# Four graph-attention layers on one core: the steps from elu to projection moved closer behind the scores

## The chip, the cores and the metric

The kernel runs on one core of a Trainium2 chip. The metric is the device time of one execution in microseconds. The median of three runs of the kernel before is 650.46 us (649.96 to 650.89). Engines are called as the profile calls them: PE (matmuls; PEld is its weight load), DVE (VectorE), ACT (ScalarE), POOL (GpSimd) and SP (SyncE, here only a queue of DMAs).

## The reference

`x` is 4096 x 64 and `adj` a 4096 x 4096 matrix of zeros and ones, dense in its first rows and columns and thin in the last. Four graph-attention layers follow each other. Cut to what matters:

```python
def layer(x, adj, W, a, slope):
    Wh = x @ W
    e = (Wh @ a_src)[:, None] + (Wh @ a_dst)[None, :]
    e = jnp.where(e > 0, e, slope * e)                 # leaky relu
    attention = softmax(where(adj > 0, e, -big), axis=1)
    return attention @ Wh                              # elu in layers 0, 2, 3; + bias in layer 1

for l in range(4):
    x = layernorm(x + elu_or_bias(layer(x, adj, W[l], a[l], slope[l])))
```

The layer norm has no weights, only mean, variance and a scaling of each row.

## The kernel before, in words

The first third of the program reads `adj` and makes for every tile of 128 rows a short list of the columns that occur in it: 85 chunks of 128 indices for 32 tiles, 12 chunks for tile 0, two or fewer new ones for each of the last twenty. A tile then attends only over its chunks. After that come the four layers, written out in full.

A layer works through 32 tiles (eight groups of four tiles) in rounds. The table `LAG` (L108) says how many rounds a step of a tile stands behind that tile's spread; a step of a group is done in the round in which its last tile is due. Every engine runs the same rounds in its own fixed order and waits on semaphores, so nothing overtakes on an engine:

- POOL, `gather` (L404): one indirect DMA for each chunk reads 128 rows of `table[l]` (the projected rows of this layer, in DRAM) into `xg`. 85 of them a layer. For layers 1 to 3, the 14 chunks called EARLY, which need rows of groups 0 to 4 alone, wait for `low_written` (the tables of groups 0 to 4); the other 71 wait for `written` (groups 5 to 7 as well). Layer 0's gathers are done during the first third.
- PE: `spread` (L572, L575) writes the scores of a tile into one of two banks and waits for the tile's gathers; `turn` (L588) transposes the exponentials; `aggregate` (L601) sums the rows; `turn_rows` (L457) and `project_rows` (L467) transpose a group of the new `x` and multiply it by the next layer's weights.
- ACT: `slope` (L716), `exponentials` (L725), `copy_turned` (L734), the elu's exponential `elu_part` (L738), `estimate_rstd` (L673, L675: a logarithm and an exponential), `copy_xt` (L667) and `copy_wh` (L660, from the projection's bank to SBUF).
- DVE: `mask_scores` (L1079, L1088), `combine` (L1103 to L1118: a group's division, residual and maximum), `norm_stats` (L1128 to L1139, the step "center"), `norm_rows` (L1147 to L1151, the step "scale"), and `slope` (L1068, the step "own"). At the start of each layer it also writes `lone_rows` in one long instruction (L1167).
- SP: as soon as a group's `copy_wh` is done, one DMA (L368) writes its rows to the next layer's table, in the order of the groups; in layer 3 it writes the result instead (L372).

In the text, "project(4)@33" means the projection of group 4 in round 33. Group g ends with tile 4g+3, so a group's step stands in round 4g+3+LAG. POOL's two waits for a layer:

```python
pool.wait_ge(low_written, 16 * l * LOW_GROUPS)
for c in EARLY:
    gather(l, TILES_OF_CHUNK[c][0], c, LOW * P)
pool.wait_ge(written, 16 * (1 + l * (GROUPS - LOW_GROUPS)))
```

## Time and profile before

| | us |
|---|---|
| median of three runs | 650.46 |
| the profiled execution, its own time | 652.01 |
| its span, first to last instruction | 649.0 |
| PE busy | 357.6 (55%) |
| DVE busy | 425.1 (66%) |
| ACT busy | 363.8 (56%) |
| POOL busy | 358.4 (55%) |

The profiled execution took 3.0 us more than its span and 1.55 us more than the median of the runs. The busy times are sums over stages of different kinds: the lists are made until about 217 us, layer 0 stands from there to about 298 us, and layers 1, 2 and 3 end at about 416, 533 and 649 us. In the slices of the page POOL is empty in layer 0, whose gathers are done by then, and works in seven to eight tenths of every slice of layers 1 to 3.

### The profile page before, as it was taken

How to read it: one execution, taken by the hardware profiler on the slowest of the kernel's cores; microseconds unless marked ns; L12 is line 12 of the kernel's file. 1: busy time of each engine (PE TensorE's matmuls, PEld its weight loads, DVE VectorE, ACT ScalarE, POOL GpSimd, SP SyncE). 2: the span in 40 equal slices, each digit the busy share in tenths (PEclk: the TensorE clock that was granted, in tenths of full speed). 3: DMA queues.
4: the chain of work that ended last, by engine and by line, in shares of the span. 5: the costliest groups of instructions: out<-in, count | busy, mean ns of one | idle time of the engine just before them, and what ended most of it. 6: DMA issues, size and time to landing. Idle time of an engine off the chain costs nothing.

```text
span 649.0 us, 10852 instructions
## 1 busy us (share of the span) xinstructions
PE 357.6 (55%) x3412; PEld 321.3 (50%) x3424; DVE 425.1 (66%) x1856; ACT 363.8 (56%) x797; POOL 358.4 (55%) x354
## 2 busy tenths in 40 slices
PE   2363322331222689872488787318866840796784
PEld 1243221221221689861477676217865830796673
DVE  2998979999999638992136567503566770346676
ACT  3574856777761379971176666206666730576563
POOL 0200574457675700017777774677777657777770
PEclk9999999999999999995599878659999875899787
DMA  7997999999981100001222221212212221222221
GB/s 269 429 380 274 369 377 408 423 413 409 410 311 19 23 5 2 27 29 42 27 28 29 36 36 35 53 26 28 29 29 44 42 52 25 28 29 35 45 43 30
DMA packets 22083, 86.73 MB, mean 134 GB/s; under 512 B 6851, under 2 KB 12102, under 8 KB 17798
## 3 DMA queue, kind: packets, MB, share of 16 engines
q1 hardware_dynamic: 10102, 73.40, 28.1%
q0 software_dynamic: 10880, 11.51, 12.4%
q10 hardware_dynamic: 1040, 1.08, 0.5%
q8 instruction: 30, 0.49, 0.3%
q14 instruction: 31, 0.25, 0.1%
HBM read 80.59 MB, written 5.37 MB: 132 GB/s over the span
## 4 chain that ended last, share of the span: by engine, by line
POOL 37%; DVE 15%; issue 14%; PE 5%; DMA 2%; ACT 2%; POOLq 0%; DVEq 0%; ACTq 0%
POOL xg L404 37%; PE bank L575 2%; DMA xg<-table,index 2%; PE bank L601 2%; DVE arena L1079 1%; DVE key L1106 1%; DVE nbr L879 1%; PE bank L588 1%; DVE penalty L999 1%; DMA table<-wh 1%; ACT arena L725 1%; DVE stats L1131 1%; ACT arena L716 1%; DVE key L866 1%; DVE top L856 1%
## 5 line engine op out<-in xcount | busy, mean ns | idle before, releaser
L404 POOL DMA_INDIRECT xg<-table,index x340 | 336.8, 990 | 191.4 <-issue 99.7
L1079 DVE CUSTOM_DVE_ANT_0 arena<-bank,arena 128x256 f32<-128x256 f32 (+3 forms) x144 | 71.4, 499 | 163.9 <-ACT arena L716 163.4
L716 ACT ACTIVATE arena<-bank,sloped_own 128x256 f32<-128x256 f32 (+3 forms) x144 | 76.9, 537 | 179.8 <-PE bank L575 179.2
L575 PE MATMUL bank<-packed,xg 128*128 128x128 f32 x744 | 120.0, 300 | 58.7 <-DMA xg<-table,index 56.9
L690 ACT ACTIVATE arena<-arena,half 128x4096 bf16<-128x4096 int32 x32 | 118.5, 3707 | 47.0 <-DMA arena<-in_adj_t 46.4
L575 PEld LDWEIGHTS bank<-packed,xg 128*128 128x128 f32 x744 | 112.7, 216 | 2.1
L601 PE MATMUL bank<-xg,arena 128*128 128x64 f32 x744 | 104.8, 279 | 0.0
L601 PEld LDWEIGHTS bank<-xg,arena 128*128 128x128 f32 x744 | 99.3, 202 | 2.0
L725 ACT ACTIVATE arena<-arena,neg_max 128x256 f32<-128x256 f32 (+3 forms) x144 | 80.7, 561 | 3.6 <-DVE neg_max L1088 3.6
L572 PEld LDWEIGHTS bank<-penalty,ident_b 128*128 128x128 bf16 x144 | 17.0, 118 | 116.8 <-DMA xg<-table,index 106.7
L588 PE MATMUL bank<-packed,arena 128*128 128x128 f32 x372 | 67.7, 290 | 10.7 <-ACT arena L734 8.2
L572 PE MATMUL bank<-penalty,ident_b 128*128 128x256 bf16 (+2 forms) x132 | 42.8, 324 | 48.8 <-DMA xg<-table,index 41.1
L398 POOL TENSOR_TENSOR colv<-word_f,packed 128x1024 f32<-128x1024 f32 (+4 forms) x10 | 21.5, 2149 | 82.1 <-DVE word_f L935 82.1
L497 PE MATMUL bank<-fix,ones_b 3*128 3x288 bf16 x32 | 13.2, 412 | 95.7 <-ACT arena L690 58.9
L734 ACT COPY arena<-bank 128x256 f32<-128x256 f32 (+3 forms) x144 | 59.7, 423 | 2.5 <-PE bank L588 2.5
L588 PEld LDWEIGHTS bank<-packed,arena 128*128 128x128 f32 x372 | 47.6, 150 | 14.3 <-ACT arena L725 13.9
L497 PEld LDWEIGHTS bank<-fix,ones_b 3*128 3x128 bf16 x32 | 3.2, 99 | 98.7 <-ACT arena L690 60.3
L467 PE MATMUL bank<-wx_pair,xt 128*128 128x132 f32 x128 | 30.3, 377 | 12.7 <-ACT wh L660 8.9
L499 PEld LDWEIGHTS bank<-packer,arena 128*128 128x128 bf16 x1024 | 29.8, 104 | 8.0 <-issue 8.0
L499 PE MATMUL bank<-packer,arena 128*128 128x9 bf16 x1024 | 32.5, 169 | 0.0
L467 PEld LDWEIGHTS bank<-wx_pair,xt 128*128 128x128 f32 x128 | 24.0, 262 | 16.2 <-issue 10.0
L1106 DVE SCALAR_TENSOR_TENSOR key<-bank,den,arena 128x64 f32<-128x64 f32 x128 | 27.5, 278 | 1.1
(128 smaller groups left out, 522.9 us busy)
## 6 DMA issues: line engine op xcount, KB each, us to landing
arena<-in_adj_t SPq DMA_DIRECT2D x32, 2048.0 KB, 12.1
xg<-table,index POOLq DMA_INDIRECT x340, 2.8
table<-wh SPq DMA_DIRECT2D x24, 132.0 KB, 1.8
table<-wh ACTq DMA_DIRECT2D x1, 1056.0 KB, 4.7
x<-in_x SPq DMA_DIRECT2D x1, 1024.0 KB, 10.4
out_x<-x SPq DMA_DIRECT2D x8, 128.0 KB, 2.2
slot_row<-in_c_slot_row SPq DMA_DIRECT2D x1, 384.0 KB, 10.8
packed<-in_c_packed SPq DMA_DIRECT2D x1, 359.0 KB
```

The lines of the kernel that those rows point to most:

```text
L404: pool.indirect_dma_start(out=xg[:, c, :], out_offset=None, in_=table[l][0:rows, :], in_offset=bass.IndirectOffsetOnAxis(ap=index[:, c:c + ...
L467: t = nc.tensor.matmul(dst[:, 2 * j * WX:2 * (j + 1) * WX], xt[:, n % 2, j * P:(j + 1) * P], wx_pair[:, l, :, :].rearrange("p a f -> p (a ...
L499: ins = nc.tensor.matmul(codes[:, c * w:(c + 1) * w], masks[:, t % 2, c * P:(c + 1) * P], packer[:, :], start=False, stop=(c == TILES - 1))
L572: nc.tensor.matmul(bank[:, 0:m * P], ident_b[:, :], penalty[:, at:at + m * P], start=True, stop=False)
L575: t = nc.tensor.matmul(bank[:, c * P:(c + 1) * P], tcol_wide(xg[:, c1 + c, TCOL:TCOL + 1]), ident[:, :], start=False, stop=(c == m - 1))
L588: t = nc.tensor.transpose(turned_ps[n % 2][:, c * P:(c + 1) * P], score[:, n % RING, c * P:(c + 1) * P], ident[:, :])
L601: t = nc.tensor.matmul(agg_ps[ng % 2][:, (k % GROUP) * F:(k % GROUP + 1) * F], slots_t[:, n % TRING, c * P:(c + 1) * P], xg[:, FIRST[k] + ...
L690: nc.scalar.activation(masks[:, t % 2, :], arena[:, t % 3, :], ACT.Sign, bias=half[:, :]).then_inc(mask_made, 1)
L716: nc.scalar.activation(score[:, n % RING, 0:m * P], score_ps[n % len(score_ps)][:, 0:m * P], ACT.Relu, bias=sloped_own[:, k:k + 1], scale= ...
L725: nc.scalar.activation(s, s, ACT.Exp, bias=neg_max[:, k:k + 1], accum_out=seg_sum[:, q:q + 1]).then_inc(exped, 1)
L734: nc.scalar.copy(slots_t[:, n % TRING, 0:m * P], turned_ps[n % 2][:, 0:m * P]).then_inc(turned_copied, 1)
L1079: nc.vector.tensor_tensor_reduce(out=y, in0=score_ps[n % len(score_ps)][:, 0:m * P], in1=y, scale=1.0, scalar=MASKED, op0=ALU.add, op1=ALU ...
```

## The change

The table sets the steps after `combine` into fewer rounds: elu from 6 to 5, center 7 to 6, rstd 8 to 6, scale 10 to 7, turn_x 11 to 8, copy_x 12 to 9, project 14 to 10, copy_wh 15 to 10, own 15 to 11. The rounds of a layer fall from 47 to 43. Within a round ACT now does copy_wh behind the slopes, and the exponentials ahead of rstd and elu. No instruction is added or taken away.

```diff
 LAG = {"spread": 0, "slope": 1, "mask": 2, "exp": 2, "turn": 3, "copy_turned": 4, "aggregate": 4,
-       "combine": 5, "elu": 6, "center": 7, "rstd": 8, "scale": 10, "turn_x": 11, "copy_x": 12,
-       "project": 14, "copy_wh": 15, "own": 15}
+       "combine": 5, "elu": 5, "center": 6, "rstd": 6, "scale": 7, "turn_x": 8, "copy_x": 9,
+       "project": 10, "copy_wh": 10, "own": 11}
...
                         for q in segs(tile_of("copy_turned", i)):
                             copy_turned(l, q)
-                        g = group_of("copy_wh", i)
-                        if g is not None and l < LAYERS - 1:
-                            copy_wh((l + 1) * GROUPS + g, g)
                         g = group_of("copy_x", i)
...
                         for q in segs(tile_of("slope", i)):
                             slope(l, q)
+                        g = group_of("copy_wh", i)
+                        if g is not None and l < LAYERS - 1:
+                            copy_wh((l + 1) * GROUPS + g, g)
+                        for q in segs(tile_of("exp", i)):
+                            exponentials(l, q)
                         g = group_of("rstd", i)
                         if g is not None:
                             estimate_rstd(g % 2, GROUP, -2.0, var_made, ln_made, rstd_made, l * GROUPS + g + 1)
                         g = group_of("elu", i)
                         if g is not None and ELU[l]:
                             elu_part(l, g)
-                        for q in segs(tile_of("exp", i)):
-                            exponentials(l, q)
```

The first place is the end of layer 0 on ACT, where the last groups are drained (L738 is the elu, L673 and L675 rstd, L734 copy_turned, L667 copy_x, L660 copy_wh). Before:

```order
L716 ACTIVATE arena<-bank,sloped_own 128x256
L725 ACTIVATE arena,seg_sum<-arena,neg_max 128x256
L734 COPY arena<-bank 128x256
L738 ACTIVATE key<-key 128x256
L725 ACTIVATE arena,seg_sum<-arena,neg_max 128x256
L734 COPY arena<-bank 128x256
L660 COPY wh<-bank 128x264
L734 COPY arena<-bank 128x256
L667 ACTIVATE xt,xsum<-bank 128x256
L673 ACTIVATE rstd<-var 128x4
L675 ACTIVATE rstd<-rstd 128x4
L738 ACTIVATE key<-key 128x256
```

Now:

```order
L716 ACTIVATE arena<-bank,sloped_own 128x256
L725 ACTIVATE arena,seg_sum<-arena,neg_max 128x256
L738 ACTIVATE key<-key 128x256
L734 COPY arena<-bank 128x256
L660 COPY wh<-bank 128x264
L725 ACTIVATE arena,seg_sum<-arena,neg_max 128x256
L673 ACTIVATE rstd<-var 128x4
L675 ACTIVATE rstd<-rstd 128x4
L734 COPY arena<-bank 128x256 x2
L667 ACTIVATE xt,xsum<-bank 128x256
L738 ACTIVATE key<-key 128x256
L660 COPY wh<-bank 128x264
```

The rstd of group 6 stood behind the last two copies of turned scores and now stands ahead of them; the copy_wh is group 4's before and group 5's now.

The second place is the same end of layer 0 on DVE (L1103 to L1115 are combine, L1128 to L1139 center, L1147 to L1151 scale; the combine is that of group 7). Before:

```order
L1139 TENSOR_TENSOR key<-key,mean_var 128x256
L1068 TENSOR_SCALAR sloped_own<-wh 128x4
L1103 TENSOR_TENSOR den<-seg_sum,lonely 128x4
L1104 RECIPROCAL den<-den 128x4
L1106 SCALAR_TENSOR_TENSOR key<-bank,den,arena 128x64 x4
L1115 SCALAR_TENSOR_TENSOR key<-key,x 128x256
L1147 TENSOR_TENSOR stat<-rstd 128x4
L1148 TENSOR_TENSOR stat<-stat,var 128x4
L1149 SCALAR_TENSOR_TENSOR stat<-stat,rstd 128x4
L1151 TENSOR_TENSOR x<-key,stat 128x256
L1128 SCALAR_TENSOR_TENSOR key<-key 128x256
```

Now:

```order
L1139 TENSOR_TENSOR key<-key,mean_var 128x256
L1147 TENSOR_TENSOR stat<-rstd 128x4
L1148 TENSOR_TENSOR stat<-stat,var 128x4
L1149 SCALAR_TENSOR_TENSOR stat<-stat,rstd 128x4
L1151 TENSOR_TENSOR x<-key,stat 128x256
L1068 TENSOR_SCALAR sloped_own<-wh 128x4
L1103 TENSOR_TENSOR den<-seg_sum,lonely 128x4
L1104 RECIPROCAL den<-den 128x4
L1106 SCALAR_TENSOR_TENSOR key<-bank,den,arena 128x64 x4
L1115 SCALAR_TENSOR_TENSOR key<-key,x 128x256
L1128 SCALAR_TENSOR_TENSOR key<-key 128x256
```

The scale of group 6 stood between the combine of group 7 and the center of group 7; it now stands ahead of both.

## Rows read from the trace of the kernel before

**Rows 1.** The page: its head line, and the chain that ended last, by engine.
```profile
span 649.0 us, 10852 instructions
...
POOL 37%; DVE 15%; issue 14%; PE 5%; DMA 2%; ACT 2%; POOLq 0%; DVEq 0%; ACTq 0%
```

**Rows 2.** The waits of POOL: line waited for, us in total, times, longest us.
```profile
POOL xg L404 <- issue: 99.7, 329, 0.3
...
POOL xg L404 <- DMA table<-wh: 78.9, 3, 61.1
```

**Rows 3.** Busy time by windows: length, then PE, PEld, DVE, ACT, POOL, clock, DMA.
```profile
230.00:290.00 60.00, 55.00 (x470) 52.03 (x470) 46.98 (x253) 49.79 (x164) 0.94 (x1) 1.00 0.04 13
...
400.00:516.00 116.00, 74.07 (x548) 68.22 (x550) 59.51 (x294) 60.71 (x190) 82.36 (x85) 0.84 0.22 35
```

**Rows 4.** The timeline at the end of layer 0: start, length, instruction, idle time before it.
```profile
273.69 0.32 SPq L368 DMA_DIRECT2D table<-wh  x1
...
278.54 0.47 ACT L716 ACTIVATE arena<-bank,sloped_own 128x256 f32<-128x256 f32 x1 [0.24 <-PE bank L575]
...
280.37 0.32 SPq L368 DMA_DIRECT2D table<-wh  x1
...
286.46 0.38 ACT L660 COPY wh<-bank 128x264 f32<-128x264 f32 x1
...
286.86 0.32 SPq L368 DMA_DIRECT2D table<-wh  x1
...
288.86 0.94 POOL L404 DMA_INDIRECT xg<-table,index  x1 [61.10 <-DMA table<-wh]
...
297.34 0.32 SPq L368 DMA_DIRECT2D table<-wh  x1
```

**Rows 5.** The timeline at the end of layer 1.
```profile
394.98 0.47 ACT L716 ACTIVATE arena<-bank,sloped_own 128x256 f32<-128x256 f32 x1 [0.96 <-PE bank L575]
...
396.92 0.94 POOL L404 DMA_INDIRECT xg<-table,index  x1 [0.30 <-issue]
...
405.54 0.32 SPq L368 DMA_DIRECT2D table<-wh  x1
...
407.53 0.95 POOL L404 DMA_INDIRECT xg<-table,index  x1 [9.67 <-DMA table<-wh]
...
415.49 0.32 SPq L368 DMA_DIRECT2D table<-wh  x1
```

**Rows 6.** The timeline at the end of layer 2.
```profile
512.85 0.47 ACT L716 ACTIVATE arena<-bank,sloped_own 128x256 f32<-128x256 f32 x1 [0.61 <-PE bank L575]
...
514.41 1.10 POOL L404 DMA_INDIRECT xg<-table,index  x1 [0.30 <-issue]
...
521.70 0.32 SPq L368 DMA_DIRECT2D table<-wh  x1
...
523.70 0.95 POOL L404 DMA_INDIRECT xg<-table,index  x1 [8.18 <-DMA table<-wh]
...
532.17 0.32 SPq L368 DMA_DIRECT2D table<-wh  x1
```

**Rows 7.** The timeline of DVE and POOL at the start of layer 2.
```profile
416.78 2.29 DVE L1167 TENSOR_TENSOR arena<-sum_wh,lonely 128x2048 f32<-128x2048 f32 x1
...
417.53 2.36 POOL L404 DMA_INDIRECT xg<-table,index  x1 [0.30 <-issue]
...
420.19 0.95 POOL L404 DMA_INDIRECT xg<-table,index  x1 [0.30 <-issue]
```

**Rows 8.** The timeline: ACT's waits in layer 0's drain, one scale in layer 1's.
```profile
289.79 0.42 ACT L738 ACTIVATE key<-key 128x256 f32<-128x256 f32 x1 [1.13 <-DVE key L1106]
...
292.85 0.20 ACT L673 ACTIVATE rstd<-var 128x4 f32<-128x4 f32 x1 [0.69 <-DVE var L1137]
...
408.81 0.17 DVE L1147 TENSOR_TENSOR stat<-rstd 128x4 f32<-128x4 f32 x1
...
409.40 0.42 DVE L1151 TENSOR_TENSOR x<-key,stat 128x256 f32<-128x256 f32 x1
```

## The prediction

> **What bounds the kernel now.** I read the chain of waits first. Of the whole span, 37% of the chain is POOL's gathers and 14% is "issue" [rows 1]; from 289 us on hardly anything else stands in it. The waits of POOL say what that is: between two gathers lie 0.30 us of its own issue, and apart from that only three waits for a table count, 78.9 us together, 61.1 the longest [rows 2]. A gather takes 0.95 us, so one every 1.25 us, and 85 of them are 106 us of each of layers 1 to 3. In the windows the other engines have room there: in 116 us of layer 2 ACT is busy 60.7 and DVE 59.5, POOL's count is the full 85 [rows 3]. So layers 1 to 3 go at POOL's pace, and what can be won is the time in which POOL does not gather: the three waits, one ahead of each layer, of which only their ends can move.
>
> The timelines show what ends them. POOL restarts 2.0 us after the table write of group 4 was issued: 286.86 to 288.86 [rows 4], 405.54 to 407.53 [rows 5], 521.70 to 523.70 [rows 6]. POOL's previous gather was over at 397.86 and 515.51, so 9.67 and 8.18 us are lost there. The reader is to see that this write belongs to copy_wh(4)@34, three rounds after the last spread: group 4's tiles were done long before, and its chain stood in the queue. Group 7's write is issued at 297.34, 415.49 and 532.17 [rows 4 to 6]; `written` is then released some 2.0 us later, and the 14 EARLY gathers (17.5 us and more) have always outlasted it.
>
> Layer 0 is another stage. Its gathers lie ready, and DVE is busy 47.0, ACT 49.8, PE 55.0 of 60 us [rows 3]. The writes come every 6.68 us, 273.69 to 280.37 [rows 4], that is 1.67 us a round.
>
> **The change part by part.** Nothing is added; everything moves. copy_wh(4) goes from round 34 to round 29, behind slope(28).
>
> *Layer 0 to 1.* slope(28) starts at 278.54 and takes 0.47 [rows 4]; copy_wh takes 0.38 and SP issues 0.02 behind it (286.46 to 286.86 [rows 4]): issue at 279.4, restart at 281.4. But by round 29 the engines now have done more of each group's work: DVE one scale more, which takes from 408.81 to 409.82, 1.0 us [rows 8], and DVE and ACT are full here. So 282.4 instead of 288.86: **6.5 us**. The bounds: 7.5 without that 1.0 us; at the other end the loss of the first rival below, 4.3 us more.
>
> *Layer 1 to 2.* slope(28) starts at 394.98, so the same steps give an issue at 395.85 and a release at 397.85. POOL is free at 397.86 and goes on 0.30 later, at 398.2 [rows 5]. The wait of 9.67 is gone, and the extra 1.0 us of DVE lies in slack. What is late next is group 7's write. The EARLY gathers would end at 398.2 + 14 x 1.25 = 415.7, while `written` comes 2.0 us behind 415.49. Group 7's own chain gets a little shorter: scale(6), 1.0 us, no longer stands between combine(7) and center(7). Against it, rstd(6) now stands on ACT ahead of the last two copy_turned, and has to wait for center(6); that is worth up to the 0.69 us that ACT waited for the same thing in the drain [rows 8]. I take the net as 0.3 us saved, so release at 417.2: a second wait of 1.2 us takes the place of the first.
>
> Then there is the long gather. Behind each restart one gather takes 2.36 to 2.86 us instead of 0.95. In layer 2 it starts at 417.53, inside the one long instruction of DVE, L1167, which runs from 416.78 to 419.07, and it ends at 419.89, 0.82 us after that instruction [rows 7]. It comes 1.29 us behind group 7's write. Before, it fell among the EARLY gathers and cost 1.41 us. Now it falls on the first gather after `written`: L1167 from 416.5 to 418.8, that gather until 419.6, the sixteenth at 419.9. Before, the sixteenth starts at 407.53 + 15 x 1.25 + 1.41 = 427.7. **7.8 us.** From there on the layer is gathers at 1.25 us in both, and all later times shift by this.
>
> The Trainium skill has a rule that speaks against this overlap (SBUF — State Buffer, section "SBUF: two separate sides"): DVE and GpSimd share a pair of ports under an exclusive lock, held for the whole instruction, also by a DVE instruction with two SBUF inputs against a GpSimd one that reads SBUF. The long gather agrees with it. By the rule the short two-input instructions of the drain (the 0.42 us of L1151) would stretch the EARLY gathers too, and these now all lie beside the drain. The trace does not bear that out: the gathers at 407.53 [rows 5] and 288.86 [rows 4] run beside a full drain and take 0.95 and 0.94. So I count the long one and give the short ones nothing; the rule's other reading is a rival.
>
> *Layer 2 to 3.* The same: issue at 513.7, POOL free at 515.51, restart at 515.8, EARLY over at 533.3, `written` at 532.17 - 0.3 + 2.0 = 533.9; L1167 ends at 535.45, that gather at 536.3, the sixteenth at 536.6. Before, 523.70 + 18.75 + 1.9 = 544.4, the 1.9 being 2.85 for 0.95. **7.8 us.**
>
> *The end of layer 3.* No table there; the drain of group 7 is shorter by the same net **0.3 us** (between nothing and 1.0).
>
> The sum is 6.5 + 7.8 + 7.8 + 0.3 = 22.4 us. Against the profiled execution (652.01, span 649.0) that is 629.6 and a span of 626.6; its time stands 1.55 above the median of the runs, so I forecast 628.1 against 650.46.
>
> **The rivals.**
>
> *Handshakes in layer 0.* elu now stands in the round of its combine and rstd in that of its center, so ACT waits for DVE with the next tiles' slopes queued behind it. Where ACT had nothing else to do it waited 1.13 us for the combine and 0.69 for the variance [rows 8], 1.8 us a group. ACT idles 10.2 us in 60 [rows 3], 1.1 us in a period of 6.68, so 0.7 us of a period is not covered; six periods before round 29 make 4.3 us, and the end of the program pays about 1 us: 633.4. Against it: exponentials now stand ahead of both, so DVE has a head start.
>
> *Group 7's drain becomes longer.* POOL now stands on group 7's write at two borders, and the order of ACT there is new. If the waits of 1.13 and 0.69 both fall on it and nothing is saved, it is some 1.3 us worse than I take at each of three places: 632.
>
> *The ports.* If each short two-input instruction of DVE holds up a gather by its 0.42 us, with some eight of them beside the EARLY gathers, 3.4 us: all of it in layer 1, less 1.2 and 0.6 of slack in the others, 8 us: 636. The Trainium skill's lock would work this way.
>
> *Slower than before.* The handshakes are paid in every layer: if ACT's wait for the combine, 1.13 us, holds up spread and turn in all 24 elu groups and POOL's gathers no longer hide it, 27 us are added: 655. It decides only if over 0.9 us of every one of those groups is exposed, though ACT has 55 us of idle time in such a layer [rows 3]. The gathers wait for no engine within a layer, which speaks against it.
>
> *Nothing moves*, since group 4's write is not what POOL waits for: that needs another releaser than the one that the timeline names three times at the same 2.0 us.
>
> **How the numbers follow.** My forecast has 0.60, handshakes 0.20, the longer drain 0.10, the ports 0.06, slower 0.02, nothing 0.01, and 0.01 for what I don't see. The predicted time is that of the likeliest. Downwards the bounds are 7.5 us at the first border, a drain shorter by the full 1.0 at each of the other two (8.5 each), 1.0 at the end: 25.5 us, 625.0; I go a little lower, to 624.2, for layer 0, where exponentials that come sooner may shorten the period. Upwards the range takes in the handshakes and the drain: 634.5. A measurement of this kernel can tell about 0.2% from no change. All cases but two lie more than that below 650.46: faster 0.97, same 0.01, slower 0.02.
>
> **What would show it.** The wait for low_written ahead of layers 2 and 3 is 0.3 us, and POOL restarts at about 282 us for layer 1. A new wait of 0.5 to 1.5 us stands 14 gathers later at two borders, with the long gather right behind it. The writes of layer 0 still come every 6.7 us. The prediction is wrong if that period grows beyond 7.2 us, if gathers beside the drain take longer than 0.95, or if PE, not POOL, stands in the chain of layers 1 to 3.

## The result: 631.87 us, and the profile after

The change takes 631.87 us (median of 4 runs, 631.13 to 632.32) against 650.21 (649.36 to 650.89, 4 runs): a ratio of 0.970, 95% interval 0.968 to 0.972. That is faster, and inside the range of 624.2 to 634.5; the predicted time, 628.1, is 3.8 us too low. The profiled execution took 631.51 us with a span of 628.5. Medians and ratios in this document leave out one execution of e5 (896.58 us) and one of f3 (1132.47 us), which took 1.5% and 31% longer than the fastest of their kernel.

The page first, with its chain by engine:

```profile
span 628.5 us, 10864 instructions
...
POOL 32%; DVE 18%; issue 12%; PE 7%; ACT 4%; DMA 2%; POOLq 0%; DVEq 0%; ACTq 0%
```

POOL and its issue still lead, but their shares fell from 37% and 14% [rows 1] to 32% and 12%, and DVE, PE and ACT gained: more of the chain now lies in layer 0 and in the drains. (The kernel is the same set of instructions; the page counts 12 more because the trace of before lacks 12 matmul records.) The waits of POOL (line waited for, us in total, times, longest):

```profile
POOL xg L404 <- issue: 100.7, 328, 1.8
...
POOL xg L404 <- DMA table<-wh: 59.1, 5, 56.2
```

Against [rows 2] the waits for a table fell from 78.9 to 59.1 us, the longest from 61.1 to 56.2. But there are five of them now, not three. A sixth pause, of 1.8 us, is counted under "issue", whose longest was 0.3 before. The timeline of POOL, the table writes and L1167 at the end of layer 0 shows where the new ones are (start, length, instruction, idle time before it):

```profile
282.87 0.32 SPq L368 DMA_DIRECT2D table<-wh  x1
...
301.06 0.32 SPq L368 DMA_DIRECT2D table<-wh  x1
302.34 2.29 DVE L1167 TENSOR_TENSOR arena<-sum_wh,lonely 128x2048 f32<-128x2048 f32 x1
303.22 2.24 POOL L404 DMA_INDIRECT xg<-table,index  x1 [0.94 <-DMA table<-wh]
305.76 0.94 POOL L404 DMA_INDIRECT xg<-table,index  x1 [0.30 <-issue]
```

Group 4's write is issued at 282.87 instead of 286.86 [rows 4]. Fourteen gathers later POOL waits again, now for group 7's write, and the gather behind that wait is the long one, since L1167 runs at the same time. The first write is issued at 255.18, so the period is (282.87 - 255.18) / 4 = 6.92 us, where it was 6.68. The same places at the end of layers 1 and 2:

```profile
391.52 0.32 SPq L368 DMA_DIRECT2D table<-wh  x1
393.51 1.03 POOL L404 DMA_INDIRECT xg<-table,index  x1 [0.37 <-DMA table<-wh]
...
409.57 0.32 SPq L368 DMA_DIRECT2D table<-wh  x1
...
412.61 1.35 POOL L404 DMA_INDIRECT xg<-table,index  x1 [1.81 <-issue]
414.26 0.94 POOL L404 DMA_INDIRECT xg<-table,index  x1 [0.30 <-issue]
...
500.43 0.32 SPq L368 DMA_DIRECT2D table<-wh  x1
...
502.43 1.00 POOL L404 DMA_INDIRECT xg<-table,index  x1 [0.35 <-DMA table<-wh]
...
519.15 0.32 SPq L368 DMA_DIRECT2D table<-wh  x1
520.44 2.29 DVE L1167 TENSOR_TENSOR arena<-sum_wh,lonely 128x2048 f32<-128x2048 f32 x1
521.17 2.38 POOL L404 DMA_INDIRECT xg<-table,index  x1 [1.25 <-DMA table<-wh]
523.85 0.94 POOL L404 DMA_INDIRECT xg<-table,index  x1 [0.30 <-issue]
```

The waits of 9.67 and 8.18 us [rows 5, 6] are now 0.37 and 0.35 us, hardly more than POOL's own issue. Second waits of 1.81 and 1.25 us stand fourteen gathers later. The 1.81 is the pause that the profile puts down to "issue": group 7's write landed at 411.54, so about 1.1 us of it come after the table was there, and what held the gather for these is not shown. They cost nothing, since the long gather ends 0.82 to 0.83 us behind L1167 at all three borders, whenever it began (305.46 for 304.63, 413.96 for 413.14, 523.55 for 522.73).

The budget of the 20.5 us between the two spans goes by marks that both traces have: the first start of L1167 (217.15 before, 218.10 now), the sixteenth gather of each layer, the last gather's end, and the end. "Saved" is the length between two marks before, less the same length now.

| stretch | before | now | saved | predicted |
|---|---|---|---|---|
| start to L1167, the lists | 217.15 | 218.10 | -0.95 | 0 |
| to layer 1's sixteenth gather | 92.38 | 87.66 | 4.7 | 6.5 |
| rest of layer 1's gathers | 88.33 | 87.38 | 0.9 | 0 |
| border 1 to 2 (last gather's end to sixteenth) | 29.84 | 21.12 | 8.7 | 7.8 |
| border 2 to 3 | 28.86 | 21.77 | 7.1 | 7.8 |
| rest of layers 2 and 3 | - | - | 0.0 | 0 |
| last gather's end to the end | 16.75 | 16.77 | 0.0 | 0.3 |
| sum | | | 20.5 | 22.4 |

### The profile page after: what moved, and what is told of

It is laid out like the page before. It is cut to its first block, busy times and chain, and to the rows that moved or that the text cites. A ratio compares the mean times of both kernels' runs of the same rounds, so it can differ in the third digit from the quotient of the medians.

```text
span 628.5 us, 10864 instructions
## 1 busy us (share of the span) xinstructions
PE 358.2 (57%) x3424; PEld 318.5 (51%) x3424; DVE 426.0 (68%) x1856; ACT 364.8 (58%) x797; POOL 355.6 (57%) x354
## 3 DMA queue, kind: packets, MB, share of 16 engines
q0 software_dynamic: 10880, 11.51, 12.9%
## 4 chain that ended last, share of the span: by engine, by line
POOL 32%; DVE 18%; issue 12%; PE 7%; ACT 4%; DMA 2%; POOLq 0%; DVEq 0%; ACTq 0%
POOL xg L404 32%; PE bank L601 2%; PE bank L575 2%; DVE key L1106 2%; DVE arena L1079 1%; DMA xg<-table,index 1%; DVE stats L1131 1%; ACT arena L716 1%; DVE nbr L879 1%; DMA table<-wh 1%; DVE mean_var L1134 1%; DVE key L1128 1%; DVE penalty L999 1%; ACT arena L734 1%; DVE key L1115 1%
## 5 line engine op out<-in xcount | busy, mean ns | idle before, releaser
L1079 DVE CUSTOM_DVE_ANT_0 arena<-bank,arena 128x256 f32<-128x256 f32 (+3 forms) x144 | 71.5, 499 | 132.5 <-ACT arena L716 132.0
L601 PE MATMUL bank<-xg,arena 128*128 128x64 f32 x744 | 105.2, 280 | 11.6 <-ACT arena L734 11.0
L601 PEld LDWEIGHTS bank<-xg,arena 128*128 128x128 f32 x744 | 98.6, 202 | 17.2 <-ACT arena L734 16.5
L572 PE MATMUL bank<-penalty,ident_b 128*128 128x256 bf16 (+3 forms) x144 | 48.7, 338 | 75.6 <-DMA xg<-table,index 70.9
L588 PE MATMUL bank<-packed,arena 128*128 128x128 f32 x372 | 65.9, 284 | 10.2 <-ACT arena L734 9.1
L572 PEld LDWEIGHTS bank<-penalty,ident_b 128*128 128x128 bf16 x144 | 17.3, 120 | 86.4 <-DMA xg<-table,index 79.9
L734 ACT COPY arena<-bank 128x256 f32<-128x256 f32 (+3 forms) x144 | 59.3, 424 | 1.3 <-PE bank L588 1.3
L588 PEld LDWEIGHTS bank<-packed,arena 128*128 128x128 f32 x372 | 46.3, 147 | 12.8 <-ACT arena L725 12.1
L467 PE MATMUL bank<-wx_pair,xt 128*128 128x132 f32 x128 | 28.9, 364 | 11.9 <-ACT wh L660 8.5
## 6 DMA issues: line engine op xcount, KB each, us to landing
x<-in_x SPq DMA_DIRECT2D x1, 1024.0 KB, 10.5
```

What stands on the lines that cost most here:

```text
L467: t = nc.tensor.matmul(dst[:, 2 * j * WX:2 * (j + 1) * WX], xt[:, n % 2, j * P:(j + 1) * P], wx_pair[:, l, :, :].rearrange("p a f -> p (a ...
L572: nc.tensor.matmul(bank[:, 0:m * P], ident_b[:, :], penalty[:, at:at + m * P], start=True, stop=False)
L588: t = nc.tensor.transpose(turned_ps[n % 2][:, c * P:(c + 1) * P], score[:, n % RING, c * P:(c + 1) * P], ident[:, :])
L601: t = nc.tensor.matmul(agg_ps[ng % 2][:, (k % GROUP) * F:(k % GROUP + 1) * F], slots_t[:, n % TRING, c * P:(c + 1) * P], xg[:, FIRST[k] + ...
L734: nc.scalar.copy(slots_t[:, n % TRING, 0:m * P], turned_ps[n % 2][:, 0:m * P]).then_inc(turned_copied, 1)
L1079: nc.vector.tensor_tensor_reduce(out=y, in0=score_ps[n % len(score_ps)][:, 0:m * P], in1=y, scale=1.0, scalar=MASKED, op0=ALU.add, op1=ALU ...
```

## The experiments

The experiments met two chips on which the kernel before takes 871 to 876 us (medians), and not 650: the record numbers them 1 and 12. It gives no number for the chip of the result, so that this was another one is my reading. e6, e7 and e8 ran on chip 12, all others on chip 1; the change itself ran again on chip 1 alone, and loses there. Each run is compared with runs of the kernel before on its own chip, each diff is against the change, and times that were expected for a chip like the first could not be tested. The first questions below are asked where the chips agree: layer 0 after its first rounds has no gathers, and its writes come every 6.69 us there with the old table of lags, as on the first chip (6.68), and every 6.92 with the new one, as on the first chip.

### Which half of the change lengthens a period of layer 0?

**e1_lag_only**: the new numbers of `LAG`, ACT's order as it was.

```diff
+                        g = group_of("copy_wh", i)
+                        if g is not None and l < LAYERS - 1:
+                            copy_wh((l + 1) * GROUPS + g, g)
...
                             slope(l, q)
-                        g = group_of("copy_wh", i)
-                        if g is not None and l < LAYERS - 1:
-                            copy_wh((l + 1) * GROUPS + g, g)
-                        for q in segs(tile_of("exp", i)):
-                            exponentials(l, q)
...
                             elu_part(l, g)
+                        for q in segs(tile_of("exp", i)):
+                            exponentials(l, q)
```

Expected:

> The new table of lags with ACT's old order in a round (copy_wh first, then copy_x, slopes, rstd, elu, exponentials last). My theory, that the change's gain is group 4's write and its shortfall (20.5 us of span instead of 22.4) is ACT waiting for DVE: now the exponentials are queued behind both waits, so layer 0's writes come every 7.2 us or slower instead of 6.9, the waits ahead of elu and rstd add up to more than in the changed kernel, and the time is 634 to 638 us. The rival, that the shortfall is only work moved ahead of round 29 and the order on ACT does not matter: 631.9 within 0.7 us, writes every 6.9 us.

Measured: 901.34 us against 871.36, ratio 1.035 (1.032 to 1.037). The writes of layer 0 come every 7.44 us: "7.2 us or slower" holds, and the rival's 6.9 does not.

**e2_order_only**: ACT's new order, the old numbers.

```diff
-       "combine": 5, "elu": 5, "center": 6, "rstd": 6, "scale": 7, "turn_x": 8, "copy_x": 9,
-       "project": 10, "copy_wh": 10, "own": 11}
+       "combine": 5, "elu": 6, "center": 7, "rstd": 8, "scale": 10, "turn_x": 11, "copy_x": 12,
+       "project": 14, "copy_wh": 15, "own": 15}
```

> The old lags with ACT's new order. My theory: nothing changes in what POOL waits for; group 4's copy_wh stays in round 34 and now stands behind the slopes, so the time is that of the kernel before or up to 1 us more: 650.2 to 651.3 us. A rival, that exponentials which come sooner shorten layer 0 by themselves: its writes come every 6.5 us or less instead of 6.68, 648 to 649 us.

Measured: 872.69 us, ratio 1.001 (1.000 to 1.003), period 6.69: no change, as expected, and not the rival's 6.5.

**e5_change_again**: the change, unaltered, as the measure for the others.

> The changed kernel, unaltered, beside the kernel before on the same chip. The four runs ahead of this one shared a chip on which the kernel before took 871 us instead of 650, with ACT idle for up to 25 us at a time wherever POOL gathers. If this run meets a chip like the first, both theories want 0.970 of the kernel before (631 to 633 against 650). If it meets one like the second, my theory is that the change loses there: EARLY gathers now lie beside the drain and slow it, so it takes 1.02 of the kernel before (886 to 894 against 871); the rival, that the change keeps its gain on any chip, wants 0.97 to 0.98.

Measured: 883.50 us against 872.49, ratio 1.013 (1.010 to 1.015). Here the change is slower than the kernel before, by little but clear of the noise. The rival of a gain on any chip is refuted; the loss that my theory wanted is there, at 1.3% and not 2%.

The waits inside three periods of layer 0, of e1 (276.6 to 299.2 us):

```profile
PE bank L588 <- ACT arena L725: 3.9, 5, 1.2
DVE arena L1079 <- ACT arena L716: 2.3, 3, 1.0
ACT rstd L673 <- DVE var L1137: 2.2, 3, 0.8
ACT key L738 <- DVE key L1106: 1.0, 3, 0.4
```

and of e5, the change (273.8 to 294.5):

```profile
PE bank L601 <- ACT arena L734: 2.4, 3, 1.0
ACT rstd L673 <- DVE var L1137: 1.7, 3, 0.8
DVE arena L1079 <- ACT arena L716: 0.8, 3, 0.5
```

The change's trace from the first chip has the same three waits with the same sums in its three periods (255.18 to 275.91), so what is learned here of layer 0 holds there. In e2 (284.1 to 304.2) no wait of PE, ACT or DVE adds up to more than 0.8 us over the three periods. So ACT's new order alone costs nothing and gives nothing. With the smaller lags ACT waits for the centring just done, 0.6 us a group; what stands behind it (copy_turned, L734) comes late, and PE's aggregate, L601, waits for that. With the exponentials still behind the rstd, PE waits for them as well and the period grows by 0.75 us instead of 0.24. The new order is what makes the short lags bearable.

### Does that wait of ACT set the period?

**e3_behind_copy**: elu (at 6) and rstd (at 7) go right behind copy_turned, ahead of the slopes; all other numbers as in the change, projection at 10.

```diff
-       "combine": 5, "elu": 5, "center": 6, "rstd": 6, "scale": 7, "turn_x": 8, "copy_x": 9,
+       "combine": 5, "elu": 6, "center": 6, "rstd": 7, "scale": 7, "turn_x": 8, "copy_x": 9,
...
                             copy_turned(l, q)
+                        g = group_of("rstd", i)
+                        if g is not None:
+                            estimate_rstd(g % 2, GROUP, -2.0, var_made, ln_made, rstd_made, l * GROUPS + g + 1)
+                        g = group_of("elu", i)
+                        if g is not None and ELU[l]:
+                            elu_part(l, g)
...
                             exponentials(l, q)
-                        g = group_of("rstd", i)
...
```

> The changed kernel with elu one round later and rstd one round later on ACT, both right behind copy_turned (elu in round 6, rstd in round 7); the steps of all other engines stay in their rounds. ACT finds combine and center done a round earlier. My theory, that ACT's waits for DVE cost 0.24 us of every period of layer 0 and hold up the last copy_turned in each drain: writes of layer 0 every 6.7 us, the last combine of layers 0, 2 and 3 0.7 us sooner or more, 628 to 630 us. The rival, that the shortfall is only work moved ahead: 631.9 within 0.7.

Measured: 879.01 us, ratio 1.009 (1.008 to 1.011); period 6.88. My theory wanted 6.7; the period hardly moved. The waits of its three periods (272.2 to 292.8):

```profile
ACT rstd L673 <- DVE var L1137: 1.1, 3, 0.4
PE bank L572 <- DVE seg_max L1079: 1.0, 2, 0.5
```

PE's wait for L734 is gone, 2.4 us, and yet only 0.1 us of three periods is gained.

**e6_rstd_later**: a full round between center and rstd, and all behind it one round later.

```diff
-       "combine": 5, "elu": 5, "center": 6, "rstd": 6, "scale": 7, "turn_x": 8, "copy_x": 9,
-       "project": 10, "copy_wh": 10, "own": 11}
+       "combine": 5, "elu": 5, "center": 6, "rstd": 7, "scale": 8, "turn_x": 9, "copy_x": 10,
+       "project": 11, "copy_wh": 11, "own": 12}
```

> The changed kernel with rstd one round later (7) and everything behind it one round later (scale 8, turn_x 9, copy_x 10, project 11, copy_wh 11, own 12), ACT's order as in the change. Layer 0 runs without gathers, so its pace can be read on either chip: writes every 6.92 us in the change, 6.69 with the old lags, 6.89 with elu and rstd behind copy_turned. My theory, that what is left of the loss is ACT waiting for the variance in the round in which DVE makes it: that wait (1.7 us in three periods) falls under 0.5 and the writes come every 6.7 us; group 4's write comes no later than in the change although it stands one round further behind. The rival, that the loss is DVE's own order: 6.9 us.

Measured: 890.32 us against 876.44, ratio 1.017 (1.014 to 1.020); the period is 7.26, the wrong way: neither my 6.7 nor the rival's 6.9. ACT does not wait for `var` any more. In its place (285.2 to 307):

```profile
ACT arena L725 <- DVE neg_max L1088: 2.0, 3, 0.7
PE bank L601 <- ACT arena L734: 1.8, 6, 0.4
...
DVE stat L1147 <- ACT rstd L675: 1.4, 3, 0.5
```

DVE now waits for ACT, and ACT for DVE's maximum. The theory that this one wait sets the period is refuted twice. DVE and ACT are each busy 18 to 19 us of 20.1 to 22.6 in all five kernels, so the period is the work of two nearly full engines plus what their waits for each other leave open. That the new lags lengthen it is shown (e2 against the change); which wait does it, and which numbers cost least, is not.

### Is the long gather the work of L1167?

**e4_split_lone**: L1167, one instruction of 128x2048, as eight of 128x256.

```diff
-                            link(nc.vector.tensor_tensor(lone_rows[:, :, :],
-                                                         sum_wh[:, :].unsqueeze(1).broadcast_to([P, TILES, F]),
-                                                         lonely[:, :].unsqueeze(2).broadcast_to([P, TILES, F]), ALU.mult))
+                            per = TILES // 8
+                            for at in range(0, TILES, per):
+                                t = nc.vector.tensor_tensor(lone_rows[:, at:at + per, :],
+                                                            sum_wh[:, :].unsqueeze(1).broadcast_to([P, per, F]),
+                                                            lonely[:, at:at + per].unsqueeze(2).broadcast_to([P, per, F]),
+                                                            ALU.mult)
+                            link(t)
```

> The changed kernel with the one long instruction of DVE at the start of a layer (128x2048, 2.29 us) written as eight of 128x256. My theory, that one gather at each border is held up by that instruction until it ends: the longest gather at a border now takes 1.4 us or less instead of 2.2 to 2.4, in layer 2 the gather behind the table no longer starts 1.8 us late, and 1.0 to 1.6 us are saved at each of three borders: 627.5 to 629 us. The rival, that the long gather only happens to stand there (it is the first after a wait, or its code is being loaded): 631.9, with a gather of 2.2 us or more at two borders.

Measured: 890.55 us, ratio 1.022 (1.021 to 1.024): the gather becomes short as expected (below), and no time is saved. **f1_split_again**, the same kernel in another set of runs:

> The change with the operation of line 1167 as eight of 128x256, on whatever chip comes. If the kernel before takes about 650 us here: the gather behind the projections' table stood 2.36, 1.35 and 2.38 us long in the profile of the change, against about 1.2 for its neighbours in this stretch, so splitting frees 1.1 + 0.2 + 1.1 = at most 2.4 us. Stretch theory: 629.5 to 631.5, ratio to before 0.968 to 0.971. Rival (the small operations hold up more gathers in turn and the wait for the table ends last): 631.5 to 634. If before takes about 870 us here: ratio 1.01 to 1.025 as in the earlier run of the same kernel (1.0223).

Measured: 888.07 us against 870.67, ratio 1.023 (1.018 to 1.027), as expected for this chip. The gather behind the table in e5:

```profile
334.97 2.36 POOL L404 DMA_INDIRECT xg<-table,index  x1 [14.16 <-DMA table<-wh]
```

and in f1:

```profile
337.59 0.76 DVE L1169 TENSOR_TENSOR arena<-sum_wh,lonely 128x256 f32<-128x256 f32 x2
338.34 1.16 POOL L404 DMA_INDIRECT xg<-table,index  x1 [14.16 <-DMA table<-wh]
339.61 0.75 DVE L1169 TENSOR_TENSOR arena<-sum_wh,lonely 128x256 f32<-128x256 f32 x2
339.80 1.04 POOL L404 DMA_INDIRECT xg<-table,index  x1 [0.30 <-issue]
```

With the instruction short, the gather is short: 1.16 and 1.04 us for 2.36 and 0.95. That holds at all three borders (at most 1.17, 1.04 and 1.18 us in e4; 2.36, 1.56 and 2.36 in e5). It is what the Trainium skill says (SBUF — State Buffer, section "SBUF: two separate sides"): DVE and GpSimd exclude each other on a shared pair of ports for the whole of an instruction. It names a DVE instruction with two SBUF inputs, as L1167 is, against a GpSimd one that reads SBUF, as the gather does (its `index`). These runs show the hold, not the ports. The short instructions cost a gather little: of the change's 42 EARLY gathers on the first chip, beside three drains, most take 0.94 to 0.96 us and the longest 1.19.

The kernel is slower all the same, and the trace says where. ACT's slopes at the start of layer 0 in f1:

```profile
234.81 0.69 ACT L716 ACTIVATE arena<-bank,sloped_own 128x512 f32<-128x512 f32 x1 [31.58 <-PE bank L575]
242.59 1.26 ACT L716 ACTIVATE arena<-bank,sloped_own 128x512 f32<-128x512 f32 x2 [7.09 <-remote]
```

In e5 the second slope comes at 236.25 after 1.51 us. POOL's last gathers of layer 0 run until 241 us; the slope waits until they are over, and layer 0's writes then stand 3.4 us later than in e5 (277.15 for 273.75). The next section shows where such waits come from. e4 and f2 have it too (7.80 and 7.09 us), and none of the eight kernels with the whole L1167 has one over 3.6 us there. In those a gather of 2.2 us, held by layer 0's L1167, thins out the gathers just then; with the split they run on. That this is why PE's signal is late only with the split is argued and was not tested.

### Why does the change lose here?

Busy time of 60 us in the middle of layer 1 (length, PE, PEld, DVE, ACT, POOL, clock, DMA share, GB/s), of the change on the first chip:

```profile
330.00:390.00 60.00, 49.17 (x381) 46.19 (x381) 37.58 (x198) 39.28 (x125) 45.38 (x49) 0.91 0.25 37
```

and of the same kernel as e5:

```profile
360.00:420.00 60.00, 6.03 (x25) 5.02 (x25) 2.35 (x10) 3.96 (x9) 45.29 (x48) 0.50 0.22 27
```

POOL gathers at the same pace, and PE, DVE and ACT do nearly nothing. They work when the gathers are over, so gathers and scores follow each other: 187 us from a layer's sixteenth gather to the next one's instead of 109 (305.76 to 414.26). The waits of e5 name a releaser that the first chip's trace does not have at all:

```profile
ACT arena L716 <- remote: 214.5, 18, 22.6
```

This line waits for PE's scores. Spreads and slopes follow each other in one order, so each slope can be matched to its spread, and the widths agree: the layer's first seven are 512, 512, 512, 512, 256, 512 and 128 columns wide on both engines. The fifth (L572 is the first matmul of the spread):

```profile
360.01 0.37 PE L572 MATMUL bank<-penalty,ident_b 128*128 128x256 bf16 x1 [7.19 <-DVE seg_max L1079]
...
390.67 0.47 ACT L716 ACTIVATE arena<-bank,sloped_own 128x256 f32<-128x256 f32 x1 [13.31 <-remote]
```

The trace's records of semaphore updates show PE's signals late: the third to seventh spread of e5's layer 1 ended at 351.09, 352.82, 361.24, 380.53 and 392.56 us and raised the semaphore at 358.42, 376.65, 390.65, 415.85 and 424.25, that is 7.3, 23.8, 29.4, 35.3 and 31.7 us later. On the first chip it is about 0.015 us, and so it is in e5 again from 437 us on, when the gathers are over. (The profile models the ends of matmuls, so it can't tell a late signal from a matmul that finished late.) ACT's and DVE's signals are prompt on both: in e5 DVE's L1079 starts 0.03 us behind a slope's end (377.39 behind 377.36), and PE's next spread 0.15 us behind DVE's maximum (378.24 behind 378.09).

**e8_paced**: some 1 us of added work on POOL (a tensor_tensor of 128x512 that changes no result) behind each gather of layers 1 to 3 that is not EARLY, in the change. Cut to the added work:

```diff
+                            nc.gpsimd.tensor_tensor(colv[:, 0:512].rearrange("p (r b) -> p r b", b=BITS),
+                                                    word_f[:, 0:32].unsqueeze(2).broadcast_to([P, 32, BITS]),
+                                                    bit_next[:, :].unsqueeze(1).broadcast_to([P, 32, BITS]),
+                                                    ALU.add).then_inc(pace, 1)
+                            paced[0] += 1
+                            pool.wait_ge(pace, paced[0])
```

> The changed kernel with about 1.2 us of other work on POOL behind each gather that is not EARLY in layers 1 to 3, so one gather every 2.5 us. Theory A, PE's signals are late only while gathers follow each other closely: the waits of ACT for the scores of over 10 us disappear, PE keeps up with the gathers, and a layer takes 20 + 71 x 2.5 + 20 = 220 us with less than 40 us between its last gather and its last write, where it is 93 us now (about 960 to 1000 us in all). Theory B, they are late whenever gathers are being made, whatever their distance: the waits stay and a layer takes 195 + 85 us, over 1080 in all. On a chip like the first: 631 + 3 x 71 x 1.25, about 890.

Measured: 916.22 us against 876.44, ratio 1.046 (1.043 to 1.048), gathers every 2.31 us. The window in the middle of its layer 1:

```profile
432.00:492.00 60.00, 34.03 (x172) 31.17 (x171) 31.98 (x110) 20.42 (x72) 51.67 (x52) 0.59 0.14 24
```

PE is busy 34 us of 60 instead of 6; e6, on this chip and without the added work, has 6.0 too (365 to 425 us). Five of the layer's eight writes (431.71 to 502.69) come while the gathers run (until 507.7), where e5 has none (its first at 460.49, its last gather over at 424.70). Behind the layer's first slope, no wait of ACT is over 7 us while these gathers run, and 26.5 us lie between its last gather and its last write, for 95.5 in e5. The signs of theory A are there and those of B are not, though the total is below both ranges (a layer takes 195 to 196 us and not 220). So it is the density of gathers that holds PE's signals back: 1.25 us apart they hardly get through, 2.31 us apart they mostly do. What in the chip does it, and why these chips and not the first, is open.

This hits the change where it gains on the first chip. It starts the EARLY gathers beside the drain; e2 (old lags) and e5, border of layers 0 and 1:

```profile
310.12 0.32 SPq L368 DMA_DIRECT2D table<-wh  x1
320.43 0.32 SPq L368 DMA_DIRECT2D table<-wh  x1
```

```profile
301.44 0.32 SPq L368 DMA_DIRECT2D table<-wh  x1
303.44 0.94 POOL L404 DMA_INDIRECT xg<-table,index  x1 [61.97 <-DMA table<-wh]
...
332.93 0.32 SPq L368 DMA_DIRECT2D table<-wh  x1
```

Counted from the first L1167, POOL restarts 7.3 us sooner in e5 (71.3 us for 78.6), but group 7's write stands 31.5 us behind group 4's, for 10.3. From the first L1167 to the sixteenth gather e5 takes 105.5 us and e2 99.2: 6.3 lost, with 3.4 and 4.3 at the other borders. That is 14.1 us; the spans differ by 12.9, since e5's lists ended 1.4 us sooner.

**e7_early_behind_table**: the EARLY gathers wait for `written` too, so none stands beside a drain.

```diff
+                    pool.wait_ge(written, 16 * (1 + l * (GROUPS - LOW_GROUPS)))
```

> The changed kernel, but the 14 EARLY gathers too wait for the tables of groups 5 to 7, so that no gather is in flight while a layer is drained. On the chip of the runs so far the change needs 31.5 us from group 4's write to group 7's in layer 0, the kernel before 10.3 us. My theory, that on this chip the signals of PE reach the others late while gathers are in flight: from group 4's write to group 7's 16 to 18 us, no ACT wait over 2 us in the drain, and since 14 gathers are then no longer hidden, 885 to 897 us in all. The rival, that the new order of steps itself makes the drain long here: 30 us again, and over 900 us. On a chip like the first: 645 to 652 us, as the gathers lose their cover.

Measured: 921.20 us against 876.44, ratio 1.051 (1.049 to 1.053). Group 7's write comes 324.63 - 305.62 = 19.0 us behind group 4's, over the 16 to 18 that I wanted but far from the rival's 30 (e5 has 31.5, and e6, on this chip, 30.2), and about as on the first chip (18.2); the longest ACT wait of the drain is 2.2 us. So the gathers do stretch the drain, and the new order of steps alone does not make it that long. The total is 24 us above the range, over the 900 of the rival. All 85 gathers, 106 us, now start only behind the last write (327.13), and since the scores do not run beside them, nothing of that is hidden.

**f3_project_12**: projection, copy and write two rounds later, half of the way back.

```diff
-       "project": 10, "copy_wh": 10, "own": 11}
+       "project": 12, "copy_wh": 12, "own": 13}
```

> The change with projection, copy and write two rounds later (12, 12, 13), half of the way back on this stage alone. If before takes about 650 us: each border loses the two rounds of a table's writer that lie between the last gather and the projection, about 2 x 1.1 to 1.7 us = 2.2 to 3.4 us where the wait for the table ends last (three borders: layer 0 to 1, 1 to 2, 2 to 3), so 638 to 642 us, ratio 0.982 to 0.987. Rival (early gathers, not the projection, end last at borders 2 and 3): only the first border loses, 634 to 636. If before takes about 870 us: the EARLY gathers start later and stretch the drain less, so the ratio lies between 1.00 and 1.02, not above that of the change, 1.0126, by more than 0.01.

Measured: 869.02 us against 870.67, ratio 0.999 (0.996 to 1.002): at the lower edge of what was expected, and no different from the kernel before. Its border 0 to 1:

```profile
305.89 0.32 SPq L368 DMA_DIRECT2D table<-wh  x1
307.89 0.94 POOL L404 DMA_INDIRECT xg<-table,index  x1 [66.81 <-DMA table<-wh]
...
326.63 0.32 SPq L368 DMA_DIRECT2D table<-wh  x1
327.93 2.29 DVE L1167 TENSOR_TENSOR arena<-sum_wh,lonely 128x2048 f32<-128x2048 f32 x1
328.65 2.38 POOL L404 DMA_INDIRECT xg<-table,index  x1 [3.59 <-DMA table<-wh]
```

Counted as above it restarts 4.8 us later than e5 (76.2 us) and yet is at the sixteenth gather 5.9 us sooner (99.6 us behind the first L1167, for 105.5), since only 20.7 us lie between the two writes. So the loss was in the overlap, not in the table's lateness. How much of the 10.8 us between 31.5 and 20.7 is less stretching, and how much the later write of group 4 itself, these runs do not separate. And the period of layer 0 is 7.05 here, longer than the change's, in the fastest kernel of the new tables: on this chip the borders decide and not the period.

**f2_behind_split**: e3 and e4 together, the candidate for a better version.

> The same and, besides, elu (6) and rstd (7) moved behind copy_turned in the round. If before takes about 650 us: with the period of layer 0 at 6.89 instead of 6.92 the handshakes give back 3 times 0.03 = 0.1 us at most, but each border is up to one round later at elu and rstd only, projection stays at 10, so nothing lost: 629.5 to 631.5. Rival (the handshakes align worse with gathers beside them, as on the chips where before takes 871 us): 632 to 634. If before takes about 870 us: ratio 1.005 to 1.02.

Measured: 881.28 us, ratio 1.015 (1.011 to 1.019), as expected for this chip. It has both parts' marks: a period of 6.88 (299.56 to 306.44), longest gathers behind the table of 1.17, 1.03 and 1.16 us, and the 7.09 us wait at layer 0's start. No version beat the kernel before on these chips, and none ran on the first one, so whether the split's shorter gathers would come through at 632 us was not measured. The expectation of f1 puts them at 2.4 us at most; it takes 2.36 for the first long gather, which is 2.24 in the trace of the change.

## Why the prediction was right, and where its terms were off

The mechanism held on the chip that it was made for: POOL's restart ahead of a layer follows group 4's write by 2.0 us (282.87 to 284.85, 391.52 to 393.51, 500.43 to 502.43), the write came sooner, and the long waits of [rows 5, 6] are gone. The times of e2 (its write at 310.12, its restart at 312.12) say the same in reverse: with the old lags the old border is back.

Of the 3.8 us between forecast and median, 1.9 are in the terms (22.4 for 20.5 of span). The other 1.9 are the step from the profiled executions to medians: the prediction set 1.55 us for it, while the profiled execution of before stands 1.80 above its new median and that of the change 0.36 below.

- **Layer 0 to 1: 6.5 predicted, 4.7 measured.** From L1167 to group 4's write 4.9 us were saved, not 6.5. The step that failed is "the writes of layer 0 still come every 6.7 us": the period is 6.92, and six of 0.24 are 1.4 us. The 0.24 is measured over four periods; that the two before the first write cost the same is an estimate. That is the rival *Handshakes in layer 0*, at a third of its price (0.7 a period, six of which are 4.2 and not 4.3), since the forecast's reason against it, exponentials ahead of both steps, is real: without them it costs 0.75 (e1). Its wait for the variance is there as well, but taking it away did not give the 0.24 back (e3, e6). The rest of the border, a second wait of 0.94 us with the long gather behind it, took 0.2 us more than the same gathers before. I had not placed this wait at this border: group 7's write comes 18.2 us behind group 4's, where it was 10.5.
- **Layer 1 to 2: 7.8 predicted, 8.7 measured.** The removed wait is as said, 9.67 to 0.37. The restart to the sixteenth gather took 20.75 us for 20.17, 0.6 longer, where I took 1.5: group 7's write came 18.05 us behind group 4's and not 19.3. The gather in L1167 took 1.35, since POOL came to it late, at 412.61, and it ended 0.82 us behind L1167, as before. The term that was mis-sized is the 0.3 us by which group 7's drain was to be shorter: from the last gather's end to group 7's write it is 16.4 us for 17.6, 1.2 less.
- **Layer 2 to 3: 7.8 predicted, 7.1 measured.** 8.18 to 0.35 as said; then 21.42 us for 20.66. The second wait is 1.25 us and not 0.6, because 18.7 us lie between the two writes and I took 18.2. It is the same term: from the last gather's end to group 7's write it is 17.1 us for 16.7, 0.4 more where I took 0.3 less. Layer 1 is the only one without an elu; whether that is why its drain alone became shorter was not tested.
- **The end: 0.3 predicted, 0.0 measured.** I weighed one scale saved (1.0) against a wait for the variance (up to 0.69). Both are there, as large as each other. The timeline of the last drain:

```profile
618.13 0.21 ACT L673 ACTIVATE rstd<-var 128x4 f32<-128x4 f32 x1 [1.01 <-DVE var L1137]
...
618.49 0.63 ACT L734 COPY arena<-bank 128x256 f32<-128x256 f32 x2
...
619.59 1.27 PE L601 MATMUL bank<-xg,arena 128*128 128x64 f32 x5
...
620.90 0.16 DVE L1103 TENSOR_TENSOR den<-seg_sum,lonely 128x4 f32<-128x4 f32 x1 [1.27 <-PE bank L601]
```

ACT waits 1.01 us for the variance, its last two copies stand behind that, then PE's aggregate, and DVE's last combine starts 9.17 us after the last gather's end, for 8.39 before. From that combine to the end it is 7.6 us for 8.4. So *Group 7's drain becomes longer* is half right: its wait is real, and just pays off the scale.
- **Not foreseen**: the rest of layer 1's gathers took 0.9 us less (before, seven of the seventy took over 1.00 us, now two; why is not traced), and the lists ended 0.95 us later, before anything that the change touches. That these two cancel is luck, and so is it that the drain's term was too small at one border and too large at the other two places: its mean over the three is 0.3, as forecast.
- ***The ports***, 0.06: no. The fourteen gathers beside a drain are longer by 0.1 to 0.3 us in all, not by 3.4; single ones take 1.03 to 1.19, which is over the 0.95 that I had set as a sign of being wrong. That sign was set too tight: some of the 71 later gathers took as much before the change too (1.16 in layers 1 and 2).
- ***Slower***, 0.02: not on the first chip. On chip 1 the change is slower (e5), but not by this mechanism: the loss is in the stretched drain. Nothing in the trace of before pointed to it, since that trace has no wait on "remote" at all.

Against the list of what would show it: the waits at borders 2 and 3 are 0.37 and 0.35 (0.3 said), the second waits 0.94, 1.81 and 1.25 (0.5 to 1.5 said, at two borders), the restart for layer 1 at 284.85 (282 said, 0.95 of it the lists), the period 6.92 (6.7 said).

## What to carry to other kernels

Where one engine only waits at stage borders, find the one write that ends its wait and count how many rounds behind its data it stands; that distance, not the busy shares, is the gain, and the next write in line is the new wait. Steps moved nearer to each other pay a little in every period in which two engines are both full, and the price is in both directions of the handshake: removing one named wait (e3, e6) gave back none of it to speak of. An overlap won on one chip can be a loss on another: measure it there before keeping it, and try the middle (12 rounds instead of 10 or 14) too.

## What the runs showed of the hardware that was not expected

- The kernel before takes 650 us in one set of runs and 871 to 876 us on chips 1 and 12. There PE's semaphore updates come 7.3 to 35.3 us late (five spreads of e5's layer 1) while POOL issues indirect gathers 1.25 us apart. ACT and DVE are answered within 0.2 us.
- With 2.31 us between gathers PE's updates mostly get through (e8: PE busy 34 of 60 us, for 6).
- A gather that meets DVE's 2.29 us instruction ends 0.82 us after it, on the first chip before and after the change (419.89 for 419.07, 413.96 for 413.14); in pieces of some 0.4 us the same work lengthens it to 1.2 us at most.
